# Loading x, context and weights channels first from the host in a decoder layer

## What is computed

```
q, k, v = x @ Wq.T + bq, x @ Wk.T + bk, x @ Wv.T + bv            # heads of 16
scores  = (q . Wq_lsr) (k . Wk_lsr)^T / sqrt(32), causal softmax
x1 = layernorm(x + (softmax @ v) @ Wo.T + bo)
a  = softmax(x1 @ wq.T @ (ctx @ wk.T)^T * scale), masked
x2 = layernorm(x1 + (a @ (ctx @ wv.T)).swap().reshape() @ Wp.T + bp)
xr, xk = mu * x2 + (1 - mu) * previous token of x2
x3 = layernorm(x2 + sigmoid(xr @ Wr.T) * (relu(xk @ Wk.T)**2 @ Wv.T))
```

## Time and profile before

| | |
|---|---|
| median of 3 runs | 1154.28 us (1152.3 to 1155.85) |
| the profiled execution | 1157.59 us |
| its span | 1155.9 us |
| mean granted TensorE clock | 0.967 |
| TensorE busy | 1052.4 us (91%), 9416 matmuls |
| VectorE busy | 727.6 us (63%) |
| ScalarE busy | 631.9 us (55%) |
| GpSimd busy | 281.3 us (24%) |
| DMA | 118.65 MB, mean 103 GB/s, 52.1% of 16 engines |

### The profile page before, as it was taken

The page is one execution under the profiler, slowest core; times in us unless marked ns, Lnnn a source line. Parts: engine busy times, 40 slices in busy tenths (PEclk is TensorE's granted clock), DMA queues, the critical chain, the costliest instruction groups (busy, mean ns, idle before and its releaser), DMA issues.

```text
span 1155.9 us, 25391 instructions
## 1 busy us (share of the span) xinstructions
PE 1052.4 (91%) x9416; PEld 820.4 (71%) x9416; DVE 727.6 (63%) x1568; ACT 631.9 (55%) x1217; POOL 281.3 (24%) x537
## 2 busy tenths in 40 slices
PE   5669899999999999999999999999999999999873
PEld 5446677777777777777777777777777777777663
DVE  3534566766666666676665666767666767676443
ACT  1124455666655556666554566665655556665642
POOL 5000122222222222222222222222222222222222
PEclk9779999999999999999998999999999999999976
DMA  6565556664555556654554656555555666453000
GB/s 161 102 116 107 100 90 115 125 124 110 104 105 105 91 113 125 125 115 106 100 113 76 117 125 125 107 110 101 103 105 99 125 125 123 103 108 52 25 10 18
DMA packets 110852, 118.65 MB, mean 103 GB/s; under 512 B 12937, under 2 KB 94347, under 8 KB 110731
## 3 DMA queue, kind: packets, MB, share of 16 engines
q1 hardware_dynamic: 110731, 117.03, 52.1%
HBM read 74.00 MB, written 41.94 MB: 100 GB/s over the span
## 4 chain that ended last, share of the span: by engine, by line
PE 65%; DMA 15%; SPq 6%; issue 5%; DVE 4%; ACT 4%; POOL 1%; ACTq 0%; POOLq 0%; DVEq 0%
PE ps_m L502 12%; PE ps_m L494 11%; DMA parts_dram<-parts 10%; PE ps_t L520 6%; PE ps_o L572 6%; PE ps_s L520 5%; SPq L353 5%; DMA stack<-parts_dram 4%; PE ps_m L465 3%; PE ps_t L526 3%; PE ps_t L531 3%; PE ps_s L526 2%; PE ps_m L474 2%; PE ps_m L632 2%; PE ps_s L531 2%
## 5 line engine op out<-in xcount | busy, mean ns | idle before, releaser
L704 ACT ACTIVATE p<-ps_t 128x1024 f32<-128x1024 f32 x192 | 196.5, 1024 | 128.5 <-PE ps_t L526 113.3
L912 DVE TENSOR_REDUCE row_max<-ps_s 128x4 f32<-128x1024 f32 (+1 forms) x192 | 232.7, 1212 | 27.7 <-PE ps_s L526 16.8
L1102 POOL TENSOR_TENSOR var<-mv,eps 128x2 f32<-128x2 f32 x96 | 18.8, 196 | 655.6 <-DVE mv L935 655.6
L520 PE MATMUL ps_s<-stack 48*128 48x128 f32 (+1 forms) x1024 | 108.9, 312 | 21.8 <-DMA stack<-parts_dram 17.2
L520 PEld LDWEIGHTS ps_t<-stack 50*128 50x128 f32 x1024 | 72.2, 187 | 57.0 <-issue 40.0
L729 ACT COPY yu<-ps_o 128x512 f32<-128x512 f32 x64 | 37.5, 586 | 136.7 <-PE ps_o L572 136.7
L520 PE MATMUL ps_t<-stack 50*128 50x128 f32 (+1 forms) x1024 | 107.8, 310 | 4.7 <-ACT p L704 2.4
L520 PEld LDWEIGHTS ps_s<-stack 48*128 48x128 f32 x1024 | 73.1, 189 | 54.7 <-DMA stack<-parts_dram 20.8
L572 PE MATMUL ps_o<-p,v_pad 128*32 128x256 f32 (+1 forms) x2048 | 97.8, 332 | 0.0
L572 PEld LDWEIGHTS ps_o<-p,v_pad 128*32 128x32 f32 x2048 | 57.9, 110 | 40.3 <-issue 18.7
L1128 POOL TENSOR_TENSOR xr_lo<-dx,xr_hi 128x512 fp32r<-128x512 f32 x32 | 40.8, 1274 | 141.5 <-ACT xr_hi L785 141.5
(11 more groups left out here) (186 smaller groups left out, 2914.1 us busy)
## 6 DMA issues: line engine op xcount, KB each, us to landing
stack<-parts_dram SPq DMA_DIRECT2D x384, 128.0 KB, 4.4
parts_dram<-parts SPq DMA_DIRECT2D x64, 512.0 KB, 5.1
x_in<-in_x SPq DMA_DIRECT2D x32, 256.0 KB, 3.0
x_res<-in_x SPq DMA_DIRECT2D x32, 256.0 KB, 3.3
out_x<-sum SPq DMA_DIRECT2D x64, 128.0 KB, 1.8
ctx_sb<-in_ctx SPq DMA_DIRECT2D x32, 120.0 KB, 5.7
stack<-shift_parts SPq DMA_DIRECT2D x128, 8.0 KB
p<-in_L_xattn_qkv_w SPq DMA_DIRECT2D x3, 256.0 KB, 5.9
```

The costliest lines, as they stand in the source:

```text
L520: nc.tensor.matmul(o, left[b.slot][r0:r0 + rows_n, h // 2, rows_at:rows_at + P], right[b.slot][r0:r0 + rows_n, h // 2, col:col + width], s ...
L704: nc.scalar.activation(p[c][:], ps_t[:], ACT.Exp).then_inc(exp_done[c], 1)
L912: nc.vector.tensor_reduce(row_max[:, tile, :, j0:j0 + nj], ps_s[:].rearrange("p (g j w) -> p g j w", j=nj, g=2), AX_X, ALU.max) \
```

## The change

The host passes x and context in a second layout, channels first (x is passed in both, since the residual needs tokens first), and all weights that had been transposed on chip already transposed. The transposes of x, of the context and of the weights go. ScalarE and VectorE take x's high and low part from the loaded tile in SBUF. The context is loaded straight into `ctxT`, which has two buffers now; the copy out of the bank goes. Wxv and Wp are loaded into their final place. Wk is split from its loaded form. The two shared banks are dealt anew: q and z1 change places, v3, vx and z2 too, and xT and ctxT leave.

```diff
-            [("xT", IN, v_["xT_lo"]), ("z1", CROSS, v_["sum1_done"]), ("x2T", FFN, a_["x2T_ready"]),
+            [("q", IN, v_["q_lo"]), ("x2T", FFN, a_["x2T_ready"]),
              ("x1T", CROSS, a_["x1T_ready"]), ("s2", CROSS, a_["a_exp_done"]), ("r3", FFN, a_["r_tanh_done"]),
-             ("mT", SCORES, v_["shift_done"]), ("v3", FFN, v_["gated_done"]), ("kx", PROBS, a_["kxT_ready"])],
-            [("yT", CROSS, v_["yT_lo"]), ("q", IN, v_["q_lo"]), ("k", IN, v_["k_lo"]),
+             ("mT", SCORES, v_["shift_done"]), ("z2", CROSS, v_["sum2_done"]), ("vx", PROBS, a_["vx_ready"])],
+            [("yT", CROSS, v_["yT_lo"]), ("z1", CROSS, v_["sum1_done"]), ("k", IN, v_["k_lo"]),
              ("v", SCORES, a_["v_ready"]), ("k3", FFN, a_["k_relu_done"]), ("g", CROSS, a_["g_ready"]),
-             ("ctxT", PROBS, a_["ctxT_ready"]), ("z2", CROSS, v_["sum2_done"]), ("vx", PROBS, a_["vx_ready"])],
+             ("v3", FFN, v_["gated_done"]), ("kx", PROBS, a_["kxT_ready"])],
...
             def load_x(b):
-                wait(sp, filled["f_xT"], b.n)
-                sp.dma_start(x_in[:], tokens(x, b.n).rearrange("(j p) c -> p j c", p=P)).then_inc(x_loaded, 16)
+                wait(sp, v_["xT_lo"], b.n)
+                sp.dma_start(x_in[:], tokens(x_turned, b.n).rearrange("(k p) t -> p k t", p=P)).then_inc(x_loaded, 16)
...
                     c = Batch(at, SCORES)
-                    wait(sp, filled["f_ctxT"], c.n)
-                    sp.dma_start(ctx_sb[:], tokens(ctx_in, c.n)).then_inc(ctx_loaded, 16)
+                    wait(sp, filled["f_vx"], c.n - 1)
+                    sp.dma_start(ctxT[c.n % 2][:], tokens(ctx_turned, c.n).rearrange("(k p) m -> p k m", p=P)) \
+                        .then_inc(ctx_loaded[c.n % 2], 16)
...
-            pe.wait_ge(ident_ready, 1)
-
             pe.wait_ge(lsr_loaded, 32)
             bank = setup_bank()
-            for s in range(2):
-                for a in range(KC):
-                    i = s * KC + a
-                    last = nc.tensor.transpose(bank[0:RANK, i * P:(i + 1) * P], lsr[:, s, a, :], ident[:])
-            last.then_inc(setup_filled, 1)
...
-            turn_weight("Wk")
...
-            pe.wait_ge(*raw_loaded["Wq"])
+            pe.wait_ge(*weight_loaded["Wq"])
             pe.wait_ge(bias_loaded, 16 * 2)
             bank = setup_bank()
-            pe.wait_ge(setup_taken, 3)
+            pe.wait_ge(setup_taken, 1)
...
             def other_weights():
-                for n in turned_names[1:]:
-                    turn_weight(n)
...
-                if on[IN]:
-                    bank = bank_free(pe, "xT", at)
-                    pe.wait_ge(x_loaded, (A.n + 1) * 16)
-                    turn_tiles(bank, x_in).then_inc(filled["f_xT"], 1)
...
-                if on[PROBS]:
-                    bank = bank_free(pe, "ctxT", at)
-                    pe.wait_ge(ctx_loaded, (Pb.n + 1) * 16)
-                    for k in range(KC):
-                        last = nc.tensor.transpose(bank[:, k * M:(k + 1) * M], ctx_sb[:, k * P:(k + 1) * P],
-                                                   ident[0:M, 0:M])
-                    last.then_inc(filled["f_ctxT"], 1)
...
                     bank = bank_free(pe, "kx", at)
-                    pe.wait_ge(a_["ctxT_ready"], Pb.n + 1)
-                    rows_out(bank, wx_fold, ctxT).then_inc(filled["f_kx"], 1)
+                    pe.wait_ge(ctx_loaded[Pb.n % 2], (Pb.n // 2 + 1) * 16)
+                    rows_out(bank, wx_fold, ctxT[Pb.n % 2]).then_inc(filled["f_kx"], 1)
...
                 if on[IN]:
-                    act.wait_ge(filled["f_xT"], A.n + 1)
+                    act.wait_ge(x_loaded, (A.n + 1) * 16)
                     wait(act, filled["f_v"], A.n - 2)
-                    nc.scalar.copy(flat(xT[A.slot][0]), bank_of("xT")[:]).then_inc(a_["xT_hi"], 1)
+                    nc.scalar.copy(flat(xT[A.slot][0]), flat(x_in)).then_inc(a_["xT_hi"], 1)
...
-                if on[PROBS]:
-                    act.wait_ge(filled["f_ctxT"], Pb.n + 1)
-                    wait(act, filled["f_vx"], Pb.n)
-                    nc.scalar.copy(flat(ctxT), bank_of("ctxT")[:, 0:KC * M]).then_inc(a_["ctxT_ready"], 1)
...
                 if on[IN]:
-                    turned_lo(A, "xT", xT[A.slot], (filled["f_v"], A.n - 2))
+                    dve.wait_ge(a_["xT_hi"], A.n + 1)
+                    wait(dve, filled["f_v"], A.n - 2)
+                    nc.vector.tensor_tensor(flat(xT[A.slot][1]), flat(x_in), flat(xT[A.slot][0]).bitcast(F32),
+                                            ALU.subtract).then_inc(v_["xT_lo"], 1)
```

More of the change, by code:

```diff
@@ L74, in decoder_layer @@
         pause = sb("pause", [P, 1])
[L75 to L84, removed]
+        raw_names = ["Wq", "Wk", "Wv", "Wo", "Wr", "Wkf", "Wvf", "Wxq", "Wxk"]
+        weight_dram = {"Wq": Wq, "Wk": WkT, "Wv": WvT, "Wo": WoT, "Wxq": Wxq, "Wxk": Wxk, "Wxv": WxvT, "Wp": WpT,
+                       "Wr": WrT, "Wkf": WkfT, "Wvf": WvfT}
+        SPLIT = ("Wk", "Wv", "Wo", "Wr", "Wkf", "Wvf")
+        wT = {n: sb("T_" + n, [P, KC, C]) for n in ("Wxv", "Wp")}
+        w_hi = {n: sb("hi_" + n, [P, KC, C], F32R) for n in ("Wq",) + SPLIT}
+        w_lo = {n: sb("lo_" + n, [P, KC, C], F32R) for n in ("Wq",) + SPLIT}
         wx_fold = sb("wx_fold", [P, KC, C])
@@ L92, in decoder_layer @@
         keep = sb("keep", [M, 1])
-        x_in = sb("x_in", [P, NT, C])
+        x_in = sb("x_in", [P, KC, T])
         xT = [[sb(f"xT_{part}{r}", [P, KC, T], F32R) for part in ("hi", "lo")] for r in range(RING)]
@@ L118, in decoder_layer @@
         yT = [sb("yT_" + part, [P, KC, T], F32R) for part in ("hi", "lo")]
-        ctx_sb = sb("ctx_sb", [M, C])
-        ctxT = sb("ctxT", [P, KC, M])
+        ctxT = [sb(f"ctxT{r}", [P, KC, M]) for r in range(2)]
         kxT = [sb(f"kxT{r}", [P, KC, M]) for r in range(RING)]
@@ L172, in sems @@
             return {n: sem(n) for n in names}
-        filled = sems(*["f_" + n for n in ("xT", "q", "k", "v", "mT", "yT", "z1", "x1T", "s2", "g", "z2", "ctxT",
+        filled = sems(*["f_" + n for n in ("q", "k", "v", "mT", "yT", "z1", "x1T", "s2", "g", "z2",
                                            "kx", "vx", "x2T", "k3", "r3", "v3", "yu")])
@@ L204, in decoder_layer @@
         shift_loaded = [sem(f"shift_loaded{r}") for r in range(RING)]
-        ctx_loaded = sem("ctx_loaded")
+        ctx_loaded = [sem(f"ctx_loaded{r}") for r in range(2)]
         x_res_loaded = sem("x_res_loaded")
@@ L303, in load_column @@
                     sp.dma_start(cols[:, i, :], v.rearrange("(a p) -> p a", p=P)).then_inc(loaded, 16)
-            for n in raw_names[:2]:
+            for n in weight_names[:2]:
                 load_weight(n)
-            sp.dma_start(x_in[:], x[0, :, :].rearrange("(j p) c -> p j c", p=P)).then_inc(x_loaded, 16)
+            sp.dma_start(x_in[:], x_turned[0, :, :].rearrange("(k p) t -> p k t", p=P)).then_inc(x_loaded, 16)
             load_column(BQ, bq, bias_loaded)
             load_column(BK, bk, bias_loaded)
-            for n in raw_names[2:]:
+            for n in weight_names[2:]:
                 load_weight(n)
@@ L386, in setup_bank @@
                 bank_no[0] += 1
-                if n >= len(setup_banks):
-                    pe.wait_ge(setup_taken, n + 1 - len(setup_banks))
-                return setup_banks[n % len(setup_banks)]
-            pe.wait_ge(ident_ready, 1)
+                return setup_banks[n]
             pe.wait_ge(lsr_loaded, 32)
             bank = setup_bank()
-            for s in range(2):
-                for a in range(KC):
-                    i = s * KC + a
-                    last = nc.tensor.transpose(bank[0:RANK, i * P:(i + 1) * P], lsr[:, s, a, :], ident[:])
-            last.then_inc(setup_filled, 1)
-            def turn_weight(n):
-                bank = setup_bank()
-                pe.wait_ge(*raw_loaded[n])
-                for k in range(KC):
[L405 to L408, removed]
-            turn_weight("Wk")
-            bank = setup_bank()
-            pe.wait_ge(setup_taken, 1)
             for a in range(KC):
@@ L681, in step @@
                     bank = bank_free(pe, "kx", at)
-                    pe.wait_ge(a_["ctxT_ready"], Pb.n + 1)
-                    rows_out(bank, wx_fold, ctxT).then_inc(filled["f_kx"], 1)
+                    pe.wait_ge(ctx_loaded[Pb.n % 2], (Pb.n // 2 + 1) * 16)
+                    rows_out(bank, wx_fold, ctxT[Pb.n % 2]).then_inc(filled["f_kx"], 1)
                 if on[PROBS]:
                     bank = bank_free(pe, "vx", at)
-                    tokens_out(bank, ctxT, wT["Wxv"], tiles=1, rows=M).then_inc(filled["f_vx"], 1)
+                    tokens_out(bank, ctxT[Pb.n % 2], wT["Wxv"], tiles=1, rows=M).then_inc(filled["f_vx"], 1)
             run_steps(step, between=other_weights)
@@ L845, in setup_take, with split, split_loaded @@
                 taken[0] += 1
-                return setup_banks[n % len(setup_banks)]
-            def split_bank(n):
```

(21 more changed lines are left out.)

51 lines of the change are left out of this document (23 added, 28 removed), and 8 rows, old and new, of the table _INS.

## The result

The changed kernel takes 1121.86 us (median of 4 runs, 1116.62 to 1122.02) beside 1153.86 us for the kernel before in the same comparison: a ratio of 0.97, with a 95% interval of 0.9671 to 0.9728. It is faster by 32.0 us; 1119.5 had been forecast.

The account below looks back on a forecast made before the run. TensorE's round per batch was taken as the bound, the transfer loop nearly as long. Full rounds 28.1, setup 2.4, early rounds 3.7 and end 0.4 made 34.6 off 1154.28: 1119.7, said as 1119.5 us; range 1107 to 1142.

Parts of the forecast that it names:

- The banks: q on TensorE, in its new bank, no longer waits for yT_lo: 1.07 us off each of 29 rounds.
- case 5: q's wait is passed on to z1 or k through the new bank neighbours: 1147 us, chance 0.07.
- The context's transposes: Two transposes leave TensorE's part without holes: 0.19 us a round, all counting; ScalarE's copy of ctxT gives nothing.
- The x transposes: Four transposes, up to 0.6 us, leave TensorE beside VectorE's longer chain: no gain, S(0) waits for the stack more often.
- x from SBUF: xT_hi and xT_lo read SBUF instead of a bank: 0.03 us a round more, on the chain, from ScalarE.
- Sum of a quiet round: A round without late transfers: 32.60 - 1.07 - 0.19 + 0.03 = 31.37 us.
- Lateness: Mean round's excess over the quiet round, from late stack and shift-row transfers: from 0.28 to 0.43 us a round.
- The context's rows of 480 B: Context load as 256 short rows delays the shift rows behind it by 0.3 us, bounds 0 to 0.6: 0.05 a round.
- Cases 3 and 4: Context load delays shift rows and Tr(0): by about 1 us, 1130.6, chance 0.15; by 2.5 us, 1168, chance 0.05.
- Setup: Path before the first q: fold starts 1.2 us earlier, x transposes take 1.12 off, 2.4 in all with small change.
- Early rounds: Rounds before 167.10 hold three of the 29 stalls: 3 x 1.23 = 3.7 us gained.
- Full rounds and end: 26 full rounds fall from 32.88 to 31.80 us, 28.1 in all; after the last q only ctx gains, 0.4.

Follow-up runs that it names:

- the last run above: Changed kernel with x split early, other loads and output stores issued behind the store of q's parts, context load behind the shift rows: 1090.37 us, ratio 0.9439.

## Why the prediction was right, and where two errors met

The sign, the size and the range were right: 1121.86 lies 2.4 above 1119.5, within 1107 to 1142. Step by step:

- **The banks: mechanism right, mis-sized.** I took the 1.07 of idle time in the row of q as what the stall costs. With the banks alone it is 1.32, since q follows S(2) by 0.58, not by the 0.84 that I had worked out as 1.91 less 1.07. Idle time is counted from a modelled end; the distance between two starts is the better measure, where a stretch shows it without the wait. z1 and k did not take the wait, so case 5 fell, and the run with the old banks shows that it would have been the whole gain.
- **The context's transposes: right.** What follows vx on TensorE starts at q+26.34 (887.37) where it was q+26.52 (852.91): 0.18 for the 0.19 that I took. That leaves nothing for ScalarE's copy, as I had said.
- **The x transposes: right.** Put back with a free bank they cost 0.01. VectorE's chain sets S(2), as I had said.
- **x from SBUF: wrong.** I added 0.03 for ScalarE and nothing for VectorE. xT_hi even started earlier, but xT_lo took 0.43 more beside GpSimd's addition. S(2) came at q+30.82 instead of q+30.54. I had priced the SBUF read by a row of ScalarE and had not asked who else runs in that window. The trace of before shows GpSimd's addition there (853.33 to 854.60), though no row of it shows what the two cost each other.
- **Sum of a quiet round:** 31.37 forecast, 31.40 measured. It is right because errors cancel: the banks gave 0.25 more and xT_hi started 0.17 earlier, xT_lo took 0.43 more. The number was better than its working.
- **Lateness:** 0.43 forecast, 0.28 measured, no more than before. S(0) and Tr(0) wait more often, as said, but part of each wait falls into time in which S(2) waits for VectorE anyway: after the q at 669.00, S(0) came 0.4 late, at q+27.71, and S(2) at q+30.80 none the less. Nor is all of the 0.28 waiting. In the 26 rounds of the changed kernel TensorE's granted clock was 1.2 GHz in two stretches (288.1 to 291.5 and 793.3 to 800.1, 10.2 us in all) and 2.4 GHz in the rest, and each of the two began behind a wait of S(0) for the stack (1.89 and 1.21 us). In the second the twelve q products took 2.56, against 1.43 at 763.49; their store was issued at q+7.49 instead of q+6, and the stack landed late again, at q+29.25. So a late landing can cost more than its wait. The chain has it:

```profile
786.15 5.61 DMA stack<-parts_dram
797.05 2.56 PE ps_m L469 x12
```

- **The context's rows of 480 B: no cost.** Of them nothing shows: the shift rows behind it land at q+28.70 where it was q+28.81. Cases 3 and 4 fell with that. The rule that I quoted from the Trainium skill's DMA: Bandwidth & Descriptors, Specifications, on transfers under 512 bytes, does not bear on the time here: the median landing is the same. Nor is the 0.6 in the minimum (2.1 to 2.7) a price of the rows, as my bound by number of rows had it: in the last run above, with the context behind the shift rows, the same 256 rows landed in 2.1 at best and 2.2 in the median.
- **Setup: gained more, kept less.** The first q came 4.0 earlier, not 2.4, because the table load moved off the path too (it waits for x_in at 6.47 now, not for the transposes at 13.32). But the second q is only 2.8 earlier (42.03 against 44.87): SyncE's first store of q's parts is at 17.82, where it was 20.85, and in the changed kernel it waits for GpSimd's constants, the last of which is this row.

```profile
17.69 0.10 POOL L1057 MEMSET x2T<- 128x2 f32 x1
```

- **Early rounds: mis-sized.** The three before the sixth q last 28.63, 30.98 and 31.41, against 28.58, 31.43 and 32.60: 1.6 gained, where I had given each the full 1.23. They are not yet full rounds, and TensorE's granted clock is lower in the first two: 0.86 and 0.95 of full speed, against 0.91 and 1.00 before. The sixth q is 4.2 earlier, where setup and early rounds together had 6.1.
- **Full rounds and end:** the 26 rounds gave 31.1 (28.1 forecast), and the end from the last q is 133.6 against 134.0, the 0.4 that I had put there. In all the span fell by 35.7 in the profiled execution, where the sum had 34.6. Here too errors cancel, 1.9 too much at the start against 3.0 too little in the rounds. And of the 35.7, 3.7 is that the profiled execution of the kernel before was slower than its median (1157.59 against 1153.86); the medians differ by 32.0.

What did not happen as the views of before suggested: removing 292 matmuls and ScalarE's 32 copies of the context bought nothing measurable in the time by itself. They lay beside something longer, or the time they freed went into a wait for a transfer or for VectorE.

## What to carry to other kernels

Where instructions of several stages share a bank in a fixed order, look at each neighbour pair for the one whose reader is late; dealing the banks anew cost nothing and gave all of the gain of this change, and a badly placed user (x behind vx) took over a third of it back. Before an operand is moved from a bank to SBUF, look which SBUF work runs on GpSimd in that window: here the layouts shortened a round only when that was out of the way, or when they let the split move into the step before. And after each shortening of a round look at the transfers again: their issue order, free before, is the next thing that pays (0.5 us a round here).

## What the runs showed of the hardware that I had not expected

- A 128x512 subtraction on VectorE with both inputs in SBUF takes 1.12 us beside a GpSimd addition of the same size, and 0.69 without it; with one input in a bank it takes 0.69 beside the same addition.
- In the setup, the copy of Wk as its high part took 1.93 us from SBUF to SBUF while GpSimd was clearing the stack (3.29 to 14.54). Five copies of the same size and form in the same trace, from 18.61 on, when GpSimd was done with it, took 0.42 each; from a bank the copy took 0.69. The subtraction right behind it (7.26, both inputs in SBUF) took 0.69 beside the clearing. So the clearing held up the copy, and not the subtraction.

```profile
5.30 1.93 DVE L809 CAST hi_Wk<-p 128x512 fp32r<-128x512 f32 x1 [0.57 <-DMA p<-in_WkT]
...
L809 DVE CAST hi_Wv<-p 128x512 fp32r<-128x512 f32 x1 | 0.4, 418 | 0.0
```

- 120 KB loaded as 256 rows of 480 B landed in the same median time as in 120 rows of 1 KB (5.7 us) behind the stack loads, and in 2.2 us when issued behind the small shift rows.
